# Moving the eviction of the transposed layer-norm tile from VectorE to ScalarE, and a ring of six PSUM banks in place of eight

## The reference, cut to what matters

```python
def _L0_attn_ref(x, ...):                      # linear recurrence between two projections
    u = jnp.einsum('bld,ed->ble', x, W_in) + b_in
    h_t = lam * h_(t-1) + gamma * u_t          # scan over the 2048 rows of a sequence
    return jnp.einsum('bld,ed->ble', y, W_out) + b_out + x

def _L0_ffn_ref(x, w1, w2):                    # activations and weights are quantized first
    h = jax.nn.gelu(_bitlinear(x, w1), approximate=False)
    return _bitlinear(h, w2)

x = x + _layernorm(_L0_attn_ref(_layernorm(x), ...))
x = x + _layernorm(_L0_ffn_ref(_layernorm(x), w1, w2))
```

## Time and profile before

| | |
|---|---|
| median of two executions | 4493.97 us |
| the profiled execution | 4513.71 us, span of its slowest core (core 4) 4512.2 us |
| the eight cores' spans | 4473.1 to 4512.2 us |
| phase A, core 4 | from about 72 us to 1527 us |
| phase B1, core 4 | to about 3560 us |
| phase B2, core 4 | to the end |
| busy: TensorE, VectorE, ScalarE | 62%, 65%, 37% |

### The profile page before, as it was taken

How to read it: one execution, slowest core, us unless ns; L and a number is a source line. 1 busy time by engine, 2 the same in 40 slices (tenths; PEclk the granted TensorE clock), 3 DMA queues, 4 the chain that set the end, 5 groups by cost and what they waited for, 6 DMA issues and landing times.

```text
span 4512.2 us, 40552 instructions; the slowest of 8 cores (4473.1 to 4512.2 us)
## 1 busy us (share of the span) xinstructions
PE 2809.8 (62%) x12080; PEld 1555.0 (34%) x12080; DVE 2941.6 (65%) x2628; ACT 1673.9 (37%) x2053; POOL 201.5 (4%) x372
## 2 busy tenths in 40 slices
PE   5665655555666345545545545545545199999998
PEld 4544444444555222212212212212212044444444
DVE  4767777677777478878878878878878322222222
ACT  1333332233444254554554554554554111111111
POOL 0000000000000000000000000000000000000000
PEclk8676766677777678778778778778778599999999
DMA  4332347567311311121122122122121566666765
GB/s 132 112 112 93 122 125 173 137 154 176 104 57 57 110 51 59 55 66 61 54 66 63 52 66 63 52 66 63 52 65 59 111 139 154 150 151 151 156 154 127
DMA packets 537185, 447.33 MB, mean 99 GB/s; under 512 B 473206, under 2 KB 473208, under 8 KB 524424
## 3 DMA queue, kind: packets, MB, share of 16 engines
q1 hardware_dynamic: 479624, 184.58, 19.3%
q0 software_dynamic: 57344, 260.15, 17.4%
HBM read 193.02 MB, written 151.00 MB: 76 GB/s over the span
## 4 chain that ended last, share of the span: by engine, by line
PE 43%; DVE 13%; DMA 5%; another core or an unknown queue 2%; issue 2%; ACT 1%; DVEq 0%; ACTq 0%; SPq 0%; POOL 0%; POOLq 0%
PE ps_h L913 23%; PE ps_f L1025 20%; DVE amh L148 6%; DMA qdT<-qd 4%; DVE bd L148 3%; DVE qd L148 2%; DVE cd L148 2%; ACT h_b L148 1%; DMA r2B<-r2scr 1%; DVE irc L148 0%; DVEq L135 0%; DVE sch_all L148 0%; DVE bn L148 0%; DVEq L834 0%
## 5 line engine op out<-in xcount | busy, mean ns | idle before, releaser
L913 PE MATMUL ps_h<-w1T,qdT 128*128 128x512 bf16 x4096 | 1030.9, 419 | 977.8 <-DMA qdT<-qd 977.8
L913 PEld LDWEIGHTS ps_h<-w1T,qdT 128*128 128x128 bf16 x4096 | 428.6, 106 | 1580.0 <-issue 1191.2
L1025 PE MATMUL ps_f<-w2T,qhT 128*128 128x512 bf16 x4096 | 886.5, 380 | 92.7 <-DMA qhT<-qhscr 92.7
L148 ACT ACTIVATE h_b<-ps_h,zerov,g3s 128x512 f32<-128x512 f32 x512 | 397.9, 777 | 568.6 <-PE ps_h L913 568.6
L1025 PEld LDWEIGHTS ps_f<-w2T,qhT 128*128 128x128 bf16 x4096 | 401.2, 98 | 577.9 <-issue 96.2
L737 PE MATMUL ps_u<-lnT,winT 128*128 128x256 f32 x2048 | 391.3, 372 | 227.5 <-ACT gu L148 189.7
L148 DVE BATCH_NORM_STATS2 bn<-ffn 128x6 f32<-128x512 f32 x128 | 88.9, 694 | 598.6 <-ACT ffn L148 591.7
L737 PEld LDWEIGHTS ps_u<-lnT,winT 128*128 128x128 f32 x2048 | 378.0, 283 | 247.1 <-issue 244.8
L148 DVE TENSOR_TENSOR bh<-y0h,r16h 128x4096 bf16<-128x4096 f32 x64 | 283.2, 4425 | 208.2 <-ACT r16h L148 208.2
L148 ACT ACTIVATE y0h<-h_b,halfv,sch_all 128x4096 f32<-128x4096 f32 x64 | 243.2, 3801 | 358.7 <-DVE sch_all L148 358.7
L148 DVE TENSOR_REDUCE amh<-h_b 128x1 f32<-128x4096 f32 x64 | 282.9, 4420 | 122.8 <-ACT h_b L148 122.8
(11 more groups left out here) (99 smaller groups left out, 2337.1 us busy)
## 6 DMA issues: line engine op xcount, KB each, us to landing
qstg<-w SPq DMA_DIRECT2D x64, 1024.0 KB, 5.9
qhscr<-qh_b POOLq DMA_DIRECT2D x64, 1024.0 KB, 5.1
x_buf<-x POOLq DMA_DIRECT2D x32, 1024.0 KB, 6.5
r2scr<-r2b POOLq DMA_DIRECT2D x64, 512.0 KB, 3.0
r2B<-r2scr POOLq DMA_DIRECT2D x64, 512.0 KB, 5.8
r2C<-r2scr POOLq DMA_DIRECT2D x64, 512.0 KB, 4.9
y<-outb POOLq DMA_DIRECT2D x64, 512.0 KB, 3.0
w1tscr<-wtp SPq DMA_DIRECT2D x32, 256.0 KB, 3.1
```

The lines of the kernel that those rows point to most:

```text
L148: ins = f(*a, **k)
L913: last = t.matmul(ps_h[q % 8][:], qdTv[ta % 2][:, j, :], w1v[:, j, 512 * hs:512 * (hs + 1)], start=(j == 0), stop=(j == DT - 1))
L1025: last = t.matmul(pslice, qhTv[ta % 2][:, j, :], w2v[:, j, 512 * half:512 * (half + 1)], start=(j == 0), stop=(j == HT - 1))
```

## The change

The loop with the four evictions of `lnT` leaves VectorE's list and stands on ScalarE's, behind the two ln1f and ahead of `ln2p(b-1)`. It is now an activation (Identity, bias from a tile of zeros, scale 1.0) with the same source, target, waits and semaphore. In B1 the ring of PSUM banks has six places in place of eight, in the allocation, in the gelus and in TensorE's wait. The lines of TensorE in phase A are unchanged.

```diff
                     if b >= 1:
                         attnp(b - 1)
-                    for gi in range(GPB):
-                        grp = GPB * b + gi
-                        tt = gi // (DT // 4)
-                        q = gi % (DT // 4)
-                        v.wait_ge(sem("s_lt"), grp + 1)
-                        if b >= 2:
-                            v.wait_ge(sem("s_u"), DT * (b - 1))
-                        ie = v.tensor_copy(
-                            lTv[b % 2][:, 4 * q:4 * q + 4, 128 * tt:128 * (tt + 1)],
-                            ps_t2[grp % 2][:].rearrange("p (q r) -> p q r", q=4))
-                        inc("s_lte", ie)
                     if b >= 1:
                         r2p(b - 1)
...
                         inc("s_ln1", i1)
+                    for gi in range(GPB):
+                        grp = GPB * b + gi
+                        tt = gi // (DT // 4)
+                        q = gi % (DT // 4)
+                        a.wait_ge(sem("s_lt"), grp + 1)
+                        if b >= 2:
+                            a.wait_ge(sem("s_u"), DT * (b - 1))
+                        ie = a.activation(
+                            lTv[b % 2][:, 4 * q:4 * q + 4, 128 * tt:128 * (tt + 1)],
+                            ps_t2[grp % 2][:].rearrange("p (q r) -> p q r", q=4),
+                            AF.Identity, bias=zerov[:], scale=1.0)
+                        inc("s_lte", ie)
                     if b >= 1:
                         ln2p(b - 1)
...
-                    for i in range(8)]
+                    for i in range(6)]
...
-                                              ps_h[q % 8][:], AF.Gelu,
+                                              ps_h[q % 6][:], AF.Gelu,
...
-                        if q >= 8:
-                            t.wait_ge(sem("s_gel"), q - 7)
+                        if q >= 6:
+                            t.wait_ge(sem("s_gel"), q - 5)
...
-                            last = t.matmul(ps_h[q % 8][:],
+                            last = t.matmul(ps_h[q % 6][:],
```

## The result

The changed kernel took 4535.0 us (median of 11 executions, lowest 4519.8) against 4495.5 us of the kernel before (10 executions, lowest 4491.3): a ratio of 1.0087, 95% interval 1.007 to 1.0103, so 0.9% slower. The forecast was 4513 us and 0.4% slower. When the changed kernel was measured once more, the ratio was 1.0056 (1.0035 to 1.0078).

What follows compares the result with a forecast made beforehand. VectorE looked like phase A's engine to relieve, but from `r2b` on each block is one chain, and `r2b` needs t2buf. Terms 19 + 0 + 0 = 19 us on the 4494 us median gave 4513 us; range 4484 to 4546.

Steps and rivals of the forecast that it cites:

- VectorE's casts hid the making of t2buf: Phase A, block 12: ScalarE finishes the first t2buf 3.3 us early, while VectorE is in its casts for 3.8 us.
- An eviction takes 0.685 us on ScalarE: Phase A: one lnT eviction estimated from the 777 ns gelu less 92 ns; bounds 0.564 and 1.203 us.
- The first r2b 0.8 us later in blocks with weight work: Phase A, blocks 1 to 23, block 0 counted the same: t2buf stands behind the evictions; 24 × 0.8 = 19 us.
- Nothing in the eight blocks without weight work: Phase A, blocks 24 to 31: r2b 0.2 us earlier or 0.3 later; −2 to +3 us in all, taken as 0.
- its better branch: Blocks 24 to 31: the clock stays high in the transposes' short pause, so r2b starts 0.2 us earlier.
- The scans could move by 16 us either way: Phase A scans: matmul pauses and their clock shift; 0.5 us a block either way, 16 us allowed.
- Six banks in B1 cost nothing: Phase B1: the first gelu ends 8 us before TensorE's seventh group needs its bank, so 0 us.
- Evictions are long, or as short as the lower bound: Phase A: at 1.203 us each, 4564 us, 12%; at 0.564 us each, part of the even-or-better rival, 18%.
- VectorE's relief reaches the end: Rival, phase A: the 3.8 us a block taken off VectorE shorten the kernel by 118 us to 4376 us; 4%.
- the second rival: Whole kernel even or a little better: short evictions, clock stays up in transposes and scans; 4486 or about 4490 us; 18%.

Runs made afterwards that it cites:

- the variants: Evictions on ScalarE between the two t2buf, 4368 us; and, against the kernel before, the casts on VectorE between the two halves of r2p, 4487 us.
- the run with the casts between the halves: The kernel before, with the four casts still on VectorE but placed between the two halves of r2p(b-1): 4487 us, ratio 0.9951.

## Why the prediction was right, point by point

- **VectorE's casts hid the making of t2buf.** Right. Six extra activations ahead of t2buf cost nothing and twelve cost 2.9 us a block where weight work stands.
- **An eviction takes 0.685 us on ScalarE.** Right: 687 ns. Taking off what a per-partition scale costs from the gelu of the same shape gave the number. `y0d` and `r16d` differ in the type that they write as well, and the gelu is another function; no run tells whether these two made no difference or happened to cancel. The 706 ns of the Trainium skill's rule (ScalarE: Activation LUTs, What ACT_TABLE_LOAD costs) are 19 ns long for this form.
- **The first r2b 0.8 us later in blocks with weight work.** Right: 0.72 us (11.04 against 10.32 from `attn_b` to `r2b`, means of eight cores over 23 blocks), 16.5 us in all. VectorE's wait has the forecast size too: from the end of `attnp` to `r2b` it is 4.6 us in blocks 1 to 23 and 3.7 in 24 to 31. Block 0 gave 0.6 us.
- **Nothing in the eight blocks without weight work.** This is the term that was mis-sized: 8 us in place of 0, where −2 to +3 had been allowed. The walk to `r2b` was right, and its better branch came true: from the end of `attnp` to `r2b` it is 3.7 us where it was 3.9, and blocks 25 to 30 came out 0.1 us shorter each where nothing else happened. What the step left out is the second projection ahead of `attnp`, whose end it left where it was, that is, at the upper clock. In block 31 and behind it, and in single other blocks, it ran at the lower one, so that on core 4 the wait of `attn_b` for ps_a rose from 35.0 to 44.5 us. That the clock was lower is shown by the rows above; why it fell there and not in the six blocks ahead is not known, and no run here isolated it.
- **The scans could move by 16 us either way.** They moved by 3 us in the changed kernel and by 1 us in its second profile, less than the cores differ among each other. The bound held here, but it did not cover what the clock can do in the scans: in the variants they moved by 40.
- **Six banks in B1 cost nothing.** Right, shown by the run with the ring alone. No core's TensorE waited for a gelu.
- **Evictions are long, or as short as the lower bound.** Both out, by 687 ns in all 128 cases.
- **VectorE's relief reaches the end.** Out for the change as it was made. Its condition, that t2buf be made first, was the right one: with it the same four evictions bring 112 and 126 us. That this is near the rival's 118 us is partly luck, since only some 70 us of the 126 come from the earlier `r2b` of blocks 1 to 23 and 40 us from the scans, which that rival did not have. The advice of the Trainium skill (TensorEngine Tiling (Array Packing), PSUM Bottleneck), to use both engines for evictions, paid with that condition and cost time without it.

In the sum: 19 us forecast; 16.5 us came where they were forecast, 8 in the blocks taken at nothing, and 3 in block 0, the scans and the rest of blocks 1 to 23, so 27.5 in phase A (25 in the second profile, by much the same shares). The mechanism was right and the size came out a third too small. Two slips in the prediction's figures change nothing: its range starts at 4484 us and calls that the second rival, whose sum is 4486; and with evictions of 0.564 us the walk of a block without weight work gives about 0.45 us earlier, not 0.6. The 39 us of the first measurement hold some 12 more that the second did not show.

## What to carry to other kernels

Before work is moved to a less busy engine, look at what stands behind its new place and how long that result lies ready before it is used: here t2buf lay ready for 3.3 us, and 4 x 0.69 us with their waits, 4.0 us at block 12, were more. Busy shares could not have told this; VectorE was rid of 88 us of work, and the kernel lost 25 to 30 us. The same move with the urgent result made first turned 0.6% slower into 2.8% faster.

## What had not been expected

The same matmuls can take half as long again or more, by the clock that TensorE is granted, and a change that only shifts work in time can change that. 32 float32 matmuls of 256 columns took 6.62 us after 6.63 us of idle time (granted clock 0.56), and 4.24 and 4.25 us after 1.23 and 0.84 us (granted clock 1.00). The pause just ahead does not tell it alone. In the run with the casts between the halves, the first 32 of the same matmuls took 5.50 us after only 1.34 us of idle time (granted clock 0.74); ahead of that lay 10.25 us of idle time, with nothing but eight transposes between. And the second projection of block 31 started after 2.0 us of idle time before and after the change, once at 1.00 and once at 0.50.

Making TensorE's earlier groups later, with no work removed or moved to another engine, took 1.7 us off each block's scans; most of it came back, in a first scan that comes 0.8 us later and in slower matmuls of the second projection (444 to 485 ns), so that the variant gained 0.5% in all.
